# Row maxima stored by ScalarE, first choices scattered first, five tiles gathered first, and the last pair routed as two groups

## What is computed

```python
logits = flat_x @ W_router + b_router              # layer 0; layer 1 without a bias
top_vals, top_idx = jax.lax.top_k(logits, TOP_K)   # TOP_K = 2 of 8 experts
...
scores = jnp.einsum('bhqd,bhkd->bhqk', q, k) / jnp.sqrt(jnp.float32(D_HEAD))
attn = jax.nn.softmax(scores, axis=-1)
out = jnp.einsum('bhqk,bhkd->bhqd', attn, v)
...
idx_flat = topi.reshape(-1)                        # layer 1: tokens sorted by expert,
sort_idx = jnp.argsort(idx_flat)                   # cut into 8 equal chunks
chunks = perm.reshape(e, n * k // e, d)
h = jax.nn.gelu(jnp.einsum('ecd,edf->ecf', chunks, w1), approximate=False)
y = jnp.einsum('ecf,efd->ecd', h, w2).reshape(n * k, d)
```

## Time and profile before

| | |
|---|---|
| median of 3 runs | 827.04 us (826.7 to 829.15) |
| profiled execution | 828.25 us, of it 826.5 us in the span of the trace |
| busy, of the span | PE 514.8 (62%), DVE 459.6 (56%), POOL 399.2 (48%), ACT 266.2 (32%) |
| chain that ended last | PE 42%, DVE 24%, issue 9%, POOL 9%, DMA 7%, SPq 5%, ACT 4% |
| TensorE's granted clock | 0.50 from 440 to 450, 0.57 from 700 to 704, 1.00 from 704 to 797 (of full speed) |

### The profile page before, as it was taken

The page is one execution under the profiler, slowest core; times in us unless marked ns, Lnnn a source line. Parts: engine busy times, 40 slices in busy tenths (PEclk is TensorE's granted clock), DMA queues, the critical chain, the costliest instruction groups (busy, mean ns, idle before and its releaser), DMA issues.

```text
span 826.5 us, 15728 instructions
## 1 busy us (share of the span) xinstructions
PE 514.8 (62%) x4535; PEld 425.2 (51%) x4536; DVE 459.6 (56%) x1523; ACT 266.2 (32%) x442; POOL 399.2 (48%) x451
## 2 busy tenths in 40 slices
PE   1687866432599999941872675464544007999960
PEld 1356663310499999830651564453433006999960
DVE  4676697984133333356961678979696901222315
ACT  0221012220144444416212575373744102222210
POOL 6212107777166666555000453285664667666660
PEclk9778867755699999985565586586665558999995
DMA  7901001144222222326244333342114113332319
GB/s 214 240 14 39 26 2 45 53 110 120 54 79 79 77 77 77 95 67 209 92 166 127 100 101 98 98 125 49 42 51 129 46 49 78 92 81 76 79 40 304
DMA packets 72421, 76.42 MB, mean 92 GB/s; under 512 B 12216, under 2 KB 60600, under 8 KB 72296
## 3 DMA queue, kind: packets, MB, share of 16 engines
q1 hardware_dynamic: 57912, 51.14, 22.8%
q0 software_dynamic: 10224, 22.40, 9.3%
q10 hardware_dynamic: 4224, 2.10, 0.8%
HBM read 46.15 MB, written 29.34 MB: 91 GB/s over the span
## 4 chain that ended last, share of the span: by engine, by line
PE 42%; DVE 24%; issue 9%; POOL 9%; DMA 7%; SPq 5%; ACT 4%; ACTq 0%; POOLq 0%; DVEq 0%
PE PS L741 38%; POOL xs L494 5%; DVE work L1259 4%; DMA work<-ys 2%; DVE XN L1282 2%; DVE stats L1264 2%; DVE X L1259 2%; SPq L576 2%; PE PS L912 2%; DVE rtmp L1259 2%; SPq L655 1%; DVE work L1687 1%; POOL work L545 1%; ACT work L1233 1%; ACT XN L1203 1%
## 5 line engine op out<-in xcount | busy, mean ns | idle before, releaser
L741 PE MATMUL PS<-work 128*128 128x36 f16 (+6 forms) x1376 | 106.8, 255 | 85.2 <-DVE work L1259 69.9
L505 POOL DMA_INDIRECT ys<-work x144 | 140.6, 977 | 34.5 <-issue 34.5
L741 PE MATMUL PS<-w,work 128*128 x1152 | 143.2, 278 | 6.7 <-issue 5.1
L741 PEld LDWEIGHTS PS<-w,work 128*128 128x128 f32 x1152 | 134.2, 192 | 13.2 <-issue 11.2
L741 PEld LDWEIGHTS PS<-work 128*128 128x128 f16 (+3 forms) x1376 | 84.6, 134 | 106.7 <-issue 73.4
L533 POOL TENSOR_TENSOR work<-XN,work 128x1024 f16<-128x1024 f32 x27 | 57.4, 2127 | 129.9 <-ACT work L1207 129.8
L1259 DVE TENSOR_TENSOR work<-PS,work 128x128 f32<-128x128 f32 (+4 forms) x130 | 51.0, 414 | 117.3 <-issue 64.6
L494 POOL DMA_INDIRECT xs<-pack,adr_i x80 | 81.5, 1018 | 62.7 <-ACT pack L1113 40.5
L741 PE MATMUL PS<-work,w1h 128*128 128x256 f16 x576 | 102.5, 280 | 1.5 <-issue 1.4
L1161 ACT ACTIVATE work<-PS,b 128x256 f32<-128x256 f32 x160 | 62.6, 475 | 102.5 <-PE PS L741 90.8
L741 PE MATMUL PS<-work,w1l 128*128 128x256 f16 x288 | 80.5, 280 | 0.0
(11 more groups left out here) (253 smaller groups left out, 828.1 us busy)
## 6 DMA issues: line engine op xcount, KB each, us to landing
work<-xs SPq DMA_DIRECT2D x132, 65.0 KB
work<-ys SPq DMA_DIRECT2D x12, 512.0 KB, 6.2
k_parts<-work SPq DMA_DIRECT2D x24, 128.0 KB
w<-k_parts SPq DMA_DIRECT2D x8, 384.0 KB
work<-q_parts SPq DMA_DIRECT2D x8, 384.0 KB
work<-k_parts SPq DMA_DIRECT2D x32, 96.0 KB
work<-q_parts SPq DMA_DIRECT2D x32, 96.0 KB
ys<-work POOLq DMA_INDIRECT x144, 2.3
```

The source lines that it names most:

```text
L505: g.indirect_dma_start(ys[l], bass.IndirectOffsetOnAxis(xin[:, q, u, :].bitcast(U32)[:, D:D + 1], 0), yrow[:, q, u, :], None).then_inc(ff[ ...
L741: return t.matmul(o, lhsT, rhs, start=start, stop=stop, skip_group_check=True)
```

## The change

Four edits, independent of each other.

1. `scatter` takes the choices as an argument. In layer 0 the four first choices of a chunk are scattered ahead of its four second choices, and the first ones wait for `pack_lo` and `ranked` only, the second ones for `packed` as before. In layer 1 the last two pairs are scattered so, a chunk at a time.
2. The stores and the load of the row maxima of chunk 0 are issued by ScalarE. Those of the other chunks stay on SP.
3. In layer 1 the last pair is routed as two groups of one chunk each, at steps 33 to 36 and 36 to 39 instead of together at 36 to 41. The table of slots waits for five groups instead of four.
4. `HEAD0` is 5 instead of 4.

```diff
-HEAD0 = 4
+HEAD0 = 5
...
+        def group(l, p):
+            return pair(p) if l == 0 or p < NP - 1 else tiles(p + NP - 1)
+
+        def group_of(l, c):
+            return c // 2 if l == 0 or c < NC - 2 else c - NP + 1
...
-        ROUTE = {"norm": (12, 20, 28, 36), "choose": (13, 21, 28, 37), "normed": (14, 22, 29, 38),
...
+        GROUPS = (NP, NP + 1)
+        ROUTE = {"norm": (12, 20, 28, 33, 36), "choose": (13, 21, 28, 34, 37), "normed": (14, 22, 29, 34, 37),
...
+        def max_stored(engine):
+            for term in range(2):
+                diag = nmax_dram[term].rearrange("j b n -> (j b) n")[0:HG * HG:HG + 1, :]
+                engine.dma_start(diag, nmaxT[64 * term:64 * term + 64, :]).then_inc(n_out, 16)
+
+        def max_loaded(engine, c):
+            engine.dma_start(qmask[96:104, c % 2, :, :, :].rearrange("p j r n -> p j (r n)"),
+                             nmax_dram.rearrange("t j b n -> (t j) b n")).then_inc(n_in, 16)
...
-            def scatter(l, c, parts=range(CT_TILES)):
-                pool.wait_ge(rt[l]["packed"], c + 1)
-                pool.wait_ge(rt[l]["ranked"], c // 2 + 1)
+            def scatter(l, c, parts=range(CT_TILES), terms=range(TOPK)):
+                pool.wait_ge(pack_lo, l * NC + c + 1)
+                if 1 in terms:
+                    pool.wait_ge(rt[l]["packed"], c + 1)
+                pool.wait_ge(rt[l]["ranked"], group_of(l, c) + 1)
                 for s in parts:
-                    for k in range(TOPK):
+                    for k in terms:
...
             for c in range(NC):
-                scatter(0, c)
+                for k in range(TOPK):
+                    scatter(0, c, terms=(k,))
...
-                if 0 <= p_ < NP:
+                if 0 <= p_ < NP - 2:
                     scatter(1, 2 * p_ + rest // CT_TILES, (rest % CT_TILES,))
+                elif NP - 2 <= p_ < NP and rest % CT_TILES == 0:
+                    for k in range(TOPK):
+                        scatter(1, 2 * p_ + rest // CT_TILES, terms=(k,))
...
             for c in range(NC):
                 if c >= 2:
                     load_blocks(c)
-                load_max(c)
-                if c == 0:
+                if c >= 1:
+                    load_max(c)
+                else:
                     for u in range(2):
                         sp.wait_ge(qk_out[u], PART_STORES * NC)
...
                     a.activation(nmaxT, PS[:, 7, 0:P // 2].bitcast(F16), ACT.Copy).then_inc(nT_sb, 1)
+                    if k == 0:
+                        act.wait_ge(nT_sb, 1)
+                        act.wait_ge(filled, 16)
+                        max_stored(act)
...
                     ins.then_inc(v9_sb, 1)
+                    if k == 0:
+                        act.wait_ge(q_blank, 1)
+                        act.wait_ge(n_out, 32)
+                        max_loaded(act, 0)
...
                 for k in route_at("norm", g):
-                    dve.wait_ge(x3_done, 2 * CT_TILES * (k + 1))
-                    norm_scale(pair(k))
+                    dve.wait_ge(x3_done, group(1, k).stop)
+                    norm_scale(group(1, k))
```

More of the change, by code:

```diff
@@ L679, in load_max @@
                 sp.wait_ge(nT_sb, c + 1)
-                if c == 0:
[L681 to L686, removed]
+                sp.wait_ge(n_in, 16 * c)
+                max_stored(sp)
                 if c >= 2:
@@ L689, in load_max @@
                 sp.wait_ge(n_out, 32 * (c + 1))
[L690 to L691 removed]
+                max_loaded(sp, c)
             def w1_load(e):
@@ L852, in route_rank @@
                     pe.wait_ge(rt[l]["count"], p)
-                sel, n = sel16[:, pair(p), :], 2 * CT_TILES
+                sel, n = sel16[:, group(l, p), :], width(group(l, p))
                 o = PS[:, BANK_RANK[l], RANK0:RANK0 + n * E].rearrange("p (s e) -> p s e", e=E)
@@ L1116, in route_exp @@
                 act.wait_ge(gap, l * NP + p + 1)
-                a.activation(wexp[:, pair(p)], wdif[:, pair(p)], ACT.Exp).then_inc(gap_exp, 1)
+                a.activation(wexp[:, group(l, p)], wdif[:, group(l, p)], ACT.Exp).then_inc(gap_exp, 1)
             for step, m, n in ORDER:
@@ L1402, in route_rows_normed @@
             def route_rows_normed(l, p):
+                t = group(l, p)
                 if l == 1 and p >= 2:
-                    dve.wait_ge(pack_hi, NC + 2 * (p - 1))
-                norm_rows(pair(p), slots(l, 2 * p).start, rt[l]["xn"])
+                    dve.wait_ge(pack_hi, NC + t.stop // CT_TILES - 4)
+                norm_rows(t, slots(l, t.start // CT_TILES).start, rt[l]["xn"])
             def route_lg(l, p):
-                t = pair(p)
+                t = group(l, p)
                 link(tt(lg[:, t, :], X[:, t, D:DE], bc(rstd[:, t], 2, E), ALU.mult))
                 if l == 0:
-                    link(tt(lg[:, t, :], lg[:, t, :], bc(brb[:], 1, 2 * CT_TILES), ALU.add))
+                    link(tt(lg[:, t, :], lg[:, t, :], bc(brb[:], 1, width(t)), ALU.add))
             def route_choose(l, p):
-                t = pair(p)
+                t = group(l, p)
                 L = lg[:, t, :]
-                a_, b_ = rtmp[:, 0, :, :], rtmp[:, 1, :, :]
-                rv = bc(rev[:], 1, 2 * CT_TILES)
+                a_, b_ = rtmp[:, 0, 0:width(t), :], rtmp[:, 1, 0:width(t), :]
+                rv = bc(rev[:], 1, width(t))
                 link(v_.tensor_reduce(rmax[:, 0, t], L, AX, ALU.max))
@@ L1467, in route_table @@
                 nl = SLOTS // P if l == 1 else 2 * TILES[0]
-                dve.wait_ge(rt[l]["rank"], NP + 1)
+                dve.wait_ge(rt[l]["rank"], GROUPS[l] + 1)
                 link(v_.tensor_copy(cnt[:], PS[:, BANK_RANK[l], TOTAL0:TOTAL0 + E]))
```

19 lines of the change are left out of this document (10 added, 9 removed).

## The result

The changed kernel takes **816.07 us** (median of 4 runs, 812.36 to 818.08), the kernel before 826.87 (4 runs, 824.16 to 829.15): a ratio of 0.987, 95% interval 0.984 to 0.990, that is 10.8 us faster, 8.3 to 13.4 by the interval. The prediction was 809.9 with a range to 815.5: right in sign, too large in size. The profiled execution of the changed kernel took 812.36 (span 810.6), the one of before 828.25 (span 826.5).

The account below looks back on a forecast made before the run. Bound by three long waits of TensorE: layer 0's scatter, the start of attention, and attention to layer 1's experts. Terms -5.0 - 7.0 - 6.9 + 1.8 = -17.1 gave 811.1 profiled, 809.9 us median; range 804.5 to 815.5.

Parts of the forecast that it names:

- I take 5.0: Layer 0 scatter: scattering first choices first starts the row about 5.1 us earlier; gain 5.0 us, bounds 4.0 to 5.5.
- Each later pair has the gate of its own addresses: Layer 0 scatter: later pairs wait for their own addresses; worked out for the last pair, this would allow 5.8 us.
- I take 7.0: Start of attention: first maxima on ScalarE's queue move tile 8's scores from 459.33 to 452.3; gain 7.0 us, bounds 4 and 10.
- with the 2.50 of the undisturbed pair, the stores land by 434.5: Start of attention: ScalarE's two maxima stores, issued at 431.5 and 432.1, land in 2.50 us, like the next chunk's stores.
- maxima landing over 5 us after their issue: Start of attention: a sign, listed beforehand, that would show the forecast wrong.
- The rival with 0.2: Start of attention: backlog on the shared DMA engines holds ScalarE's stores too; gain 4 instead of 7, total 813; chance 0.2.
- now all go about 1 us earlier: Start of attention: SP issues chunk 2's loads about 1 us earlier; they are there at 452, letting tile 8 start at 452.3.
- 6.9 gained: End of layer 1's attention: routing the last pair as two groups starts gathers at 668.0 instead of 674.89; bounds 5 to 7.3.
- cost +1.8: Head of layer 1's experts: gathering five tiles first idles away the tile done early, costing 1.8 us (0.3 to 3).
- The rival that it gains 3.3: Head of layer 1's experts: tile 6 isn't late, so the edit gives -3.3 instead of +1.8; total 804.8; chance 0.08.
- The table did not end the wait: Rival, end of layer 1's attention: the two groups delay the table, which ends the wait; gain 3, total 813.8; chance 0.12.
- TensorE's clock did come back: Rival, layer 1's experts: clock stays low after the longer stall, 1.45 us more per tile, up to 847.6; chance 0.03.

Follow-up runs that it names:

- e7: Changed kernel with SP's last six query stores held until the first maxima are loaded, chunk 2's loads staying behind all query stores; ratio 0.994 to the kernel before (disturbed batch).
- e10: The changed kernel, unedited, as base of its batch; ratio 0.9865 to the kernel before.
- e14: e13 with four tiles gathered first instead of five; 809.97 us, ratio 0.980 to the kernel before.
- e9: Changed kernel with SP waiting for the first maxima's load, then issuing chunk 2's loads, then the last six query stores; ratio 0.987 to the kernel before.
- e6: Changed kernel with SP issuing chunk 2's loads, then waiting for the first maxima's load, then the last six query stores; ratio 0.988 to the kernel before (disturbed batch).
- e13: e9 with the first w1 load moved forward and the wait for all query stores behind chunk 1's maxima; ratio 0.984 to the kernel before.

## Why the prediction was right in sign and too large

The forecast sum of -17.1 stands against -12.9 from these traces and -10.8 and -11.1 in the medians. No single edit went another way; three gains came out a sixth to a third smaller than forecast. The misses are 1.7, 1.6 and 1.2 us.

- **Edit 1, "I take 5.0".** The start gave 4.4 (1.08 behind the addresses instead of 5.52), not 5.1: the step from the written addresses to the first scatter was 0.9 us, not 0.2. The main step that failed is "Each later pair has the gate of its own addresses": I worked it out for the last pair alone, where it allows 5.8. The second pair's allows less. With a start this early 16 scatters are through before its addresses are written, hence the 1.56 us wait at 140.79, at which 3.5 of the gain are left (146.13 - 119.71 before, 140.79 - 117.86 now). Of 4.0 at the last scatter 3.3 reach attention; why not all is open.
- **Edit 2, "I take 7.0".** This is where the mechanism was wrong. The step that failed is "with the 2.50 of the undisturbed pair, the stores land by 434.5". B and C of the table took 6.2 and 6.4 instead of about 4 and 4, and a sign of being wrong, "maxima landing over 5 us after their issue", came true. The rival with 0.2 was the true mechanism, though its 4 us was too small: 5.4. A second step failed with it, "now all go about 1 us earlier": the gate behind the maxima, chunk 2's loads, is real (e7) and still ends the wait of tile 8, by 0.46 us, but it came 22.8 us behind the transposed maxima, where the forecast had 21.2 (452.3 - 431.06). The late maxima alone would have put tile 8 at 22.4. So either failure takes most of the 1.6 us that are missing, and they don't add. The Trainium skill (DMA: Bandwidth & Descriptors, Issuing engines are not separate DMA queues) speaks for what B and C show; I let its neighbour (Queues, rings and completion order) speak for the small stores getting through, and 3.03 us (e7) against 6.30 (e10) is against that reading.
- **Edit 3, "6.9 gained".** Right step by step: packs, table 3.4 us later behind the add of step 33, landing as gate. Counted from the add of step 33 (at 630.93 in the trace of before, 619.44 now) the last scatter is 0.8 later than drawn up, 654.09 + 11.49 = 665.6 instead of 664.8, by irregular scatters (1.43, 1.23 and 1.14 instead of 0.97) in the row that now gates; and the interval in the trace of before was itself 0.5 longer than in the two other traces without the edit. Only the size of the term was off, by 1.2.
- **Edit 4, "cost +1.8".** Confirmed with its mechanism, +1.5 to the end and +1.9 to the last scatter of a result. One tile more ahead of the stall is idled away (the waits of 2.81 and 3.39 us), and the kept rows are later. The rival that it gains 3.3 fell.
- **The base.** The trace of before was a late one and that of after an early one: their first addresses are at 119.71 and 117.86, and over the profiles of undisturbed batches they lie at 117.8 to 118.0, 119.7 to 120.1 and 122.5, for kernels whose instructions up to there are the same. Comparing the two traces alone gave -15.9 and would have seemed to confirm the forecast. What the start depends on was not tried.
- **Other rivals.** The table did not end the wait in the changed kernel (it was done 2.7 us ahead of the first gather; the forecast had table and landing within 1 us). TensorE's clock did come back. Behind the stall it was granted 0.60 from 688 to 693, the first block, and 1.00 from 693 to 697 and to 775, as before within one tile. Over the whole stretch it was 0.93 in both:

```profile
674.00:797.00 123.00, 111.03 (x1007) 102.07 (x1008) 29.20 (x92) 34.04 (x33) 81.62 (x109) 0.93 0.29 75
```

```profile
674.00:797.00 123.00, 102.74 (x952) 95.77 (x950) 31.64 (x95) 30.24 (x30) 73.76 (x102) 0.93 0.31 88
```

(the clock is the third figure from the end.)

- **Slips in the working.** VectorE is free 2.0 us ahead of the add at 634.04, not 1.4, and 655.8 + 7 x 1.27 is 664.7; neither moves the sum.

What stays open is why edit 1 alone gives 6.4 us in the medians and 3.3 in the traces, and edit 2 3.2 and 5.4. The interval of edit 1's median, 4.7 to 8.1, leaves out the traces' figure; that of edit 2's, 1.0 to 5.5, just holds it.

## What to carry to other kernels

In this kernel, moving a small urgent transfer to another engine's queue saved the issue time but not the wait behind large transfers already started. What helped was to keep the first queue silent for some microseconds ahead of it (4.6 us in e7). Then look for what that silence makes late, since the gain is only kept once the next gate is moved too. When a row of waiting work is pulled forward, check the gate of every member, the second above all, not only the last. And measure an edit inside a trace, from the event ahead of it to the event behind it, over several traces; the distance between two whole executions holds the luck of both.

## What the runs showed of the hardware

- The same kernel took 826 to 827 us in some batches and 883 to 885 in others, with the same granted clock (0.74 to 0.78): in the changed kernel TensorE was idle on nothing named for 61 us instead of 6, in single waits of up to 19 us and in stretches with single matmuls 1.41 us apart. All eight profiles of those batches have waits put down to another core or an unknown queue, the ten others none. Two batches on chips of the same number, 14, fell on either side, so it isn't shown to be the chip. The cause is open.
- Two stores of 16 KB on ScalarE's queue took 3.0 us from issue until the load that waits for them was issued when SP's queue had been silent for 4.6 to 4.9 us (e7, e14), and 5.8 us when it had ended the issue of 384 KB of stores 1.3 us earlier (e9).
- SP issued the same six query stores in 8.4 to 9.1 us right behind three others, and in 3.8 to 4.5 us when no store had been issued for 11 us or more (e6, e7, e9, e13, e14), though in e9, e13 and e14 the loads of chunk 2 stood right ahead of them.
